# A two-layer graph network on one core: Q and K as three float32r matmuls on split operands, with a new order of events

## What is computed

```python
def euler_step(h, _):
    ax = jnp.einsum('nm,bmd->bnd', adj_mx, h)
    f = alph * 0.5 * (ax - h) + h @ w_eff - h + x0
    return (h + dt * f, None)
...
qkv = h @ W
...
scores = jnp.einsum('bhid,bhjd->bhij', q, k) / np.sqrt(HEAD_DIM) + mask
attn = jax.nn.softmax(scores, axis=-1)
out = jnp.einsum('bhij,bhjd->bhid', attn, v)
...
x = _layernorm(x + _L0_gnn_ref(x, adj, ...), axis=-1)
x = _layernorm(x + _L1_gnn_ref(x, L1_gnn_W, adj), axis=-1)
```

## Time and profile before

| | |
|---|---|
| median of three runs | 652.85 us (652.73 to 653.16) |
| the profiled execution | 653.2 us, its span 651.4 us |
| PE busy | 622.8 us, 96% of the span |
| DVE busy | 520.5 us, 80% |
| ACT busy | 452.5 us, 69% |
| Pool busy | 146.5 us, 22% |
| mean granted TensorE clock | 0.988 of full speed |

### The profile page before, as it was taken

How to read it: one execution, slowest core, us unless ns; L and a number is a source line. 1 busy time by engine, 2 the same in 40 slices (tenths; PEclk the granted TensorE clock), 3 DMA queues, 4 the chain that set the end, 5 groups by cost and what they waited for, 6 DMA issues and landing times.

```text
span 651.4 us, 11315 instructions
## 1 busy us (share of the span) xinstructions
PE 622.8 (96%) x3083; PEld 434.2 (67%) x3083; DVE 520.5 (80%) x1406; ACT 452.5 (69%) x1025; POOL 146.5 (22%) x170
## 2 busy tenths in 40 slices
...
DMA packets 38141, 35.55 MB, mean 55 GB/s; under 512 B 8064, under 2 KB 25312, under 8 KB 38112
## 3 DMA queue, kind: packets, MB, share of 16 engines
...
...
## 4 chain that ended last, share of the span: by engine, by line
PE 87%; DVE 6%; POOL 3%; issue 2%; ACT 1%; DMA 0%; POOLq 0%; SPq 0%; DVEq 0%
PE psL L932 9%; PE psL L933 9%; PE psL L934 9%; PE psE L1032 9%; PE psO L1060 9%; PE psS L946 8%; PE psL L922 5%; PE psL L924 5%; PE psL L923 5%; PE psM L1006 5%; PE psM L1011 2%; PE psL L997 2%; DVE ET L1301 2%; PE psE L848 2%; PE psS L848 2%
## 5 line engine op out<-in xcount | busy, mean ns | idle before, releaser
L1247 DVE CUSTOM_DVE_ANT_0 Sm<-psS,mask 128x512 f32<-128x512 f32 x256 | 172.3, 686 | 30.4 <-PE psS L946 22.6
L737 ACT ACTIVATE Sm<-Sm,negmax 128x512 f32<-128x512 f32 x240 | 171.4, 716 | 24.6 <-DVE negmax L1247 24.1
L1301 DVE TENSOR_TENSOR ET<-psE,maskT 128x512 f32<-128x512 f32 x232 | 154.4, 683 | 13.4 <-PE psE L1032 12.7
L784 ACT ACTIVATE ET<-ET 128x512 f32<-128x512 f32 x240 | 144.2, 620 | 19.3 <-DVE ET L1301 19.1
L946 PE MATMUL psS<-Ks,Qs 96*128 96x512 f32 x256 | 102.4, 432 | 4.6 <-DMA Ks<-kl 2.3
L650 POOL TENSOR_TENSOR rstd<-var,minus_half 128x4 f32<-128x4 f32 x32 | 32.8, 1025 | 307.0 <-DVE var L1230 307.0
L1032 PE MATMUL psE<-Qs,Ks 98*128 98x512 f32 x232 | 94.2, 454 | 2.1 <-DVE ET L1301 0.5
L1032 PEld LDWEIGHTS psE<-Qs,Ks 98*128 98x128 f32 x232 | 42.9, 190 | 33.9 <-issue 13.2
L1060 PE MATMUL psO<-ET,V 128*32 128x512 f32 x512 | 65.4, 608 | 0.0
L946 PEld LDWEIGHTS psS<-Ks,Qs 96*128 96x128 f32 x256 | 48.7, 192 | 20.1 <-issue 6.3
L922 PE MATMUL psL<-z,Rh 128*128 128x512 f32 x144 | 57.6, 400 | 0.0
...
## 6 DMA issues: line engine op xcount, KB each, us to landing
Qs<-qh SPq DMA_DIRECT2D x128, 64.0 KB, 2.0
Ks<-kh SPq DMA_DIRECT2D x128, 64.0 KB, 2.0
...
Qs<-Mh SPq DMA_DIRECT2D x30, 4.0 KB
```

What stands on the lines that cost most here:

```text
L737: nc.scalar.activation(E[:, slot % 2, i, :] if moved(a, h) else row, row, ACT.Exp, scale=-1.0, bias=negmax[:, h * NT + i:h * NT + i + 1], ...
L784: nc.scalar.activation(ET[:, n, i, :], ET[:, n, i, :], ACT.Exp, scale=SCALE).then_inc(st_exp, 1)
L1247: V_.tensor_tensor_reduce(out=Sm[:, i % 2, :], in0=psS[i % 2][:, :], in1=mask[:, i, :], scale=-SCALE, scalar=3e38, op0=ALU.add, op1=ALU.mi ...
L1301: V_.tensor_tensor(ET[:, n, i, :], e_bank(b, n, i)[:, :], maskT[:, i, :], ALU.add).then_inc(t_ev[i % 2], 1)
```

## The change

W's columns for Q and K are split once in the setup into Wh (ACT) and Wl (DVE). The transposed x1 is no longer copied out whole: ACT takes its high part x1Th, DVE its low part x1Tl (a new event XL, which now frees psM for Q), and Q and K are three float32r matmuls each. V still needs the whole x1T: Pool adds it up from the two parts (a new event X1S), and V waits for that. The lists of events are rewritten. Below are the lists of the loop on PE, DVE, Pool and SP, and the code; ACT's list and those for fill and drain are left out.

```diff
...
 PE_EVENTS = [
-    ("TR", 0, 1, 2), ("Z", 1, 0, 0), ("S", 3, 0, 2), ("X1T", 0, 0, 1), ("S", 3, 1, 2), ("TR", 0, 2, 2),
-    ("TR", 0, 3, 2), ("CB", 0, 0, 3), ("Q", 1, 0, 1), ("XT", 0, 0, 0), ("S", 3, 2, 2), ("Z", 2, 0, 0),
-    ("TR", 1, 0, 2), ("K", 2, 0, 1), ("TR", 1, 1, 2), ("TR", 1, 2, 2), ("S", 3, 3, 2), ("C", 2, 0, 0),
-    ("MT", 1, 0, 2), ("TR", 1, 3, 2), ("C", 1, 0, 0), ("S", 0, 0, 1), ("YT", 0, 0, 0), ("S", 0, 1, 1),
-    ("V", 3, 0, 1), ("TR", 2, 0, 2), ("TR", 2, 1, 2), ("S", 0, 2, 1), ("S", 0, 3, 1), ("J", 0, 0, 0),
-    ("TR", 2, 2, 2), ("TR", 2, 3, 2), ("S", 1, 0, 1), ("S", 1, 1, 1), ("TR", 3, 0, 2), ("C", 0, 0, 0),
-    ("S", 1, 2, 1), ("YT", 1, 0, 0), ("S", 1, 3, 1), ("TR", 3, 1, 2), ("TR", 3, 2, 2), ("PV", 0, 0, 2),
-    ("MT", 0, 0, 1), ("TR", 3, 3, 2), ("S", 2, 0, 1), ("S", 2, 1, 1), ("J", 1, 0, 0), ("PV", 1, 0, 2),
-    ("UT", 0, 0, 0), ("S", 2, 2, 1), ("PV", 2, 0, 2), ("PV", 3, 0, 2), ("TR", 0, 0, 1), ("S", 2, 3, 1),
+    ("S", 2, 2, 2), ("TR", 0, 0, 2), ("S", 2, 3, 2), ("Z", 1, 0, 0), ("TR", 0, 1, 2), ("X1T", 0, 0, 1),
+    ("S", 3, 0, 2), ("S", 3, 1, 2), ("TR", 0, 2, 2), ("CB", 0, 0, 3), ("TR", 0, 3, 2), ("XT", 0, 0, 0),
+    ("Q", 1, 0, 1), ("Z", 2, 0, 0), ("TR", 1, 0, 2), ("S", 3, 2, 2), ("K", 2, 0, 1), ("S", 3, 3, 2),
+    ("TR", 1, 1, 2), ("TR", 1, 2, 2), ("C", 2, 0, 0), ("MT", 1, 0, 2), ("C", 1, 0, 0), ("TR", 1, 3, 2),
+    ("S", 0, 0, 1), ("YT", 0, 0, 0), ("S", 0, 1, 1), ("V", 3, 0, 1), ("S", 0, 2, 1), ("TR", 2, 0, 2),
+    ("TR", 2, 1, 2), ("S", 0, 3, 1), ("J", 0, 0, 0), ("TR", 2, 2, 2), ("TR", 2, 3, 2), ("S", 1, 0, 1),
+    ("S", 1, 1, 1), ("TR", 3, 0, 2), ("C", 0, 0, 0), ("S", 1, 2, 1), ("TR", 3, 1, 2), ("S", 1, 3, 1),
+    ("YT", 1, 0, 0), ("TR", 3, 2, 2), ("PV", 0, 0, 2), ("MT", 0, 0, 1), ("TR", 3, 3, 2), ("S", 2, 0, 1),
+    ("S", 2, 1, 1), ("J", 1, 0, 0), ("PV", 1, 0, 2), ("UT", 0, 0, 0), ("PV", 2, 0, 2), ("PV", 3, 0, 2),
 ]
...
 DVE_EVENTS = [
-    ("S", 2, 1, 2), ("LN1A", 0, 0, 1), ("S", 2, 2, 2), ("TR", 0, 0, 2), ("S", 2, 3, 2), ("LN1B", 0, 0, 1),
-    ("TR", 0, 1, 2), ("Z", 1, 0, 0), ("S", 3, 0, 2), ("TR", 0, 2, 2), ("S", 3, 1, 2), ("CB", 0, 0, 3),
-    ("QL", 1, 0, 1), ("S", 3, 2, 2), ("TR", 0, 3, 2), ("XT", 0, 0, 0), ("TR", 1, 0, 2), ("Z", 2, 0, 0),
-    ("KL", 2, 0, 1), ("S", 3, 3, 2), ("TR", 1, 1, 2), ("TR", 1, 2, 2), ("MT", 1, 0, 2), ("LN2A", 0, 0, 3),
-    ("TR", 1, 3, 2), ("S", 0, 0, 1), ("S", 0, 1, 1), ("YT", 0, 0, 0), ("S", 0, 2, 1), ("S", 0, 3, 1),
-    ("TR", 2, 0, 2), ("TR", 2, 1, 2), ("TR", 2, 2, 2), ("S", 1, 0, 1), ("S", 1, 1, 1), ("TR", 2, 3, 2),
-    ("TR", 3, 0, 2), ("S", 1, 2, 1), ("S", 1, 3, 1), ("TR", 3, 1, 2), ("YT", 1, 0, 0), ("MT", 0, 0, 1),
-    ("TR", 3, 2, 2), ("TR", 3, 3, 2), ("S", 2, 0, 1), ("J", 1, 0, 0),
+    ("TR", 0, 0, 2), ("LN1B", 0, 0, 1), ("S", 2, 3, 2), ("TR", 0, 1, 2), ("Z", 1, 0, 0), ("XL", 0, 0, 1),
+    ("TR", 0, 2, 2), ("S", 3, 0, 2), ("TR", 0, 3, 2), ("CB", 0, 0, 3), ("S", 3, 1, 2), ("QL", 1, 0, 1),
+    ("XT", 0, 0, 0), ("TR", 1, 0, 2), ("S", 3, 2, 2), ("KL", 2, 0, 1), ("Z", 2, 0, 0), ("S", 3, 3, 2),
+    ("TR", 1, 1, 2), ("TR", 1, 2, 2), ("MT", 1, 0, 2), ("LN2A", 0, 0, 3), ("TR", 1, 3, 2), ("S", 0, 0, 1),
+    ("S", 0, 1, 1), ("YT", 0, 0, 0), ("S", 0, 2, 1), ("S", 0, 3, 1), ("TR", 2, 0, 2), ("TR", 2, 1, 2),
+    ("TR", 2, 2, 2), ("S", 1, 0, 1), ("TR", 2, 3, 2), ("S", 1, 1, 1), ("TR", 3, 0, 2), ("S", 1, 2, 1),
+    ("S", 1, 3, 1), ("TR", 3, 1, 2), ("YT", 1, 0, 0), ("TR", 3, 2, 2), ("S", 2, 0, 1), ("MT", 0, 0, 1),
+    ("J", 1, 0, 0), ("TR", 3, 3, 2), ("S", 2, 1, 1), ("LN1A", 0, 0, 0), ("S", 2, 2, 1),
 ]
...
 POOL_EVENTS = [
-    ("KEEP", 0, 0, 2), ("LN1A", 0, 0, 1), ("ADD", 0, 0, 3), ("LN2A", 0, 0, 3), ("XS", 0, 0, 0),
+    ("XS", 0, 0, 0), ("LN2A", 0, 0, 3), ("LN1A", 0, 0, 0), ("ADD", 0, 0, 2), ("X1S", 0, 0, 0), ("KEEP", 0, 0, 0),
 ]
...
 SP_EVENTS = [
-    ("STK", 2, 0, 2), ("MT", 0, 0, 2), ("STK", 3, 0, 2), ("XIN", 0, 0, 0), ("OUT", 0, 0, 4), ("STK", 0, 0, 1),
-    ("MT", 1, 0, 2), ("STK", 1, 0, 1),
+    ("STK", 1, 0, 2), ("XIN", 0, 0, 0), ("STK", 2, 0, 2), ("MT", 0, 0, 2), ("STK", 3, 0, 2), ("STK", 0, 0, 1),
+    ("OUT", 0, 0, 4), ("MT", 1, 0, 2),
 ]
...
+        Wh = sb("Wh", [P, 2 * D], F32R)
+        Wl = sb("Wl", [P, 2 * D], F32R)
...
+        x1Th = sb("x1Th", [P, N], F32R)
+        x1Tl = sb("x1Tl", [P, N], F32R)
...
@@ -670,6 +679,11 @@
                             ins = nc.gpsimd.tensor_scalar(y[:, t, :], att[:, t, :], mv[:, 1, t, 0:1],
                                                           rstd[:, 1, t:t + 1], ALU.subtract, ALU.mult)
                         ins.then_inc(y_done, 1)
+                    elif kind == "X1S":
+                        pool.wait_ge(m_ev, MPB * b + 1)
+                        if after_first(b):
+                            pool.wait_ge(m_mm, MPB * b)
+                        nc.gpsimd.tensor_tensor(x1T[:, :], f(x1Th[:, :]), f(x1Tl[:, :]), ALU.add).then_inc(x1t_sum, 1)
                     elif kind == "KEEP":
                         pool.wait_ge(x1_done, b + 1)
                         if not isinstance(b, int) or b > 1:
@@ -723,6 +737,9 @@
                 act.wait_ge(r_ev, q1)
                 nc.scalar.activation(Rh[:, q0:q1, :], Rf[:, q0:q1, 0:D], ACT.Copy).then_inc(rt_hi, 1)
             power_high(2, 2)
+
+            act.wait_ge(in_qkv, 16)
+            nc.scalar.activation(Wh[:, :], W_sb[:, 0:2 * D], ACT.Copy).then_inc(w_hi, 1)
 
             def high(bank_ap, dst):
                 return nc.scalar.activation(dst, bank_ap, ACT.Copy)
@@ -758,7 +775,7 @@
                         nc.scalar.activation(YT[:, :], psL[bank][:, :], ACT.Copy).then_inc(l0_ev[bank], 1)
                     elif kind == "X1T":
                         act.wait_ge(m_mm, MPB * b + 1)
-                        nc.scalar.activation(x1T[:, :], psM[:, :], ACT.Copy).then_inc(m_ev, 1)
+                        high(psM[:, :], x1Th[:, :]).then_inc(x1t_hi, 1)
                     elif kind in ("Q", "K"):
                         act.wait_ge(m_mm, MPB * b + n + 1)
                         if kind == "Q" and after_first(b):
@@ -1003,9 +1020,14 @@
                         last.then_inc(m_mm, 1)
                     elif kind in ("Q", "K"):
                         cols = slice(0, D) if kind == "Q" else slice(D, 2 * D)
-                        mm(psM[:, :], W_sb[:, cols], x1T[:, :], start=True, stop=True).then_inc(m_mm, 1)
+                        if kind == "Q" and isinstance(b, int) and b == 0:
+                            pe.wait_ge(w_lo, 1)
+                        mm(psM[:, :], Wh[:, cols], x1Th[:, :], start=True, stop=False)
+                        mm(psM[:, :], Wl[:, cols], x1Th[:, :], start=False, stop=False)
+                        mm(psM[:, :], Wh[:, cols], x1Tl[:, :], start=False, stop=True).then_inc(m_mm, 1)
                     elif kind == "V":
                         cols = slice(2 * D, 3 * D)
+                        pe.wait_ge(x1t_sum, b + 1)
                         for t in range(NT):
                             nodes = slice(t * P, (t + 1) * P)
                             last = mm(psM[:, nodes], x1T[:, nodes], W_sb[:, cols], start=True, stop=True)
@@ -1209,6 +1231,8 @@
             power_low(2, 2)
             mask_columns(3)
             dve.wait_ge(c_vec, 5 + NT)
+            dve.wait_ge(w_hi, 1)
+            V_.tensor_tensor(Wl[:, :], W_sb[:, 0:2 * D], f(Wh[:, :]), ALU.subtract).then_inc(w_lo, 1)
             V_.memset(y[:, :, :], 0.0).then_inc(y_out, Y_FREE)
             V_.memset(negmax[:, :], 0.0).then_inc(c_ev, C_FREE)
 
@@ -1282,6 +1306,9 @@
                         dve.wait_ge(x1_kept, b)
                         normalise(0, b, lambda t: psM[:, t * P:(t + 1) * P],
                                   lambda t: x1[:, t, :]).then_inc(x1_done, 1)
+                    elif kind == "XL":
+                        dve.wait_ge(x1t_hi, b + 1)
+                        low(psM[:, :], x1Th[:, :], x1Tl[:, :]).then_inc(m_ev, 1)
                     elif kind in ("QL", "KL"):
                         dve.wait_ge(m_hi, (MPB - 2) * b + n)
                         h_, l_ = {"QL": (qh, ql), "KL": (kh, kl)}[kind]
```

22 lines of the change are left out of this document (12 added, 10 removed), and 301 rows, old and new, of tables (ACT_DRAIN, ACT_EVENTS, ACT_FILL, DVE_DRAIN).

## The result

The changed kernel takes 655.29 us (median of 22 executions, 651.82 to 657.58), the kernel before in the same session 653.18 (22 executions, 652.07 to 654.00). The ratio is 1.0025, with a 95% interval of 1.0013 to 1.0037: slower by a quarter of a per cent, where 650.8 us was forecast. The time lies 0.3 us above the range given.

A forecast was written before the change was run, and what follows sets the result against it. PE was taken as the bound, nearly without a stall, with DVE's chain nearly as long. Loop -1.0, fill -0.8, other orders -0.4, loop and drain entries -0.1, drain +0.3: -2.0 us, giving 650.8 us, range 646.5 to 655.0.

The forecast's parts named there:

- Loop: Ten loop batches: DVE's queue eats most of PE's 0.45 us gain, leaving 0.1 a batch; -1.0 us, -2.2 to +1.0.
- the queue from TR(0,1) on: Loop, DVE from TR(0,1) to YT's low part: works without a gap, ends at 21.55 us and sets J's start.
- The kl row of the prediction: Loop, DVE's waits ahead of J: 0.1 us of the vanishing waits left in because kh comes only just in time.
- The rival in which PE alone sets the pace: Loop: DVE stretch too long by 0.3 us or more, period 34.9; -6.5 us, 646.3 us in all, chance 0.15.
- The new waits: Loop: Q for XL (slack 0.1 us), K and C's third part near zero, V for Pool; no cost.
- the third rival: Drain clock: another 5 us at half clock gives 653.3 us, chance 0.10; staying at 2.4 GHz gives 648.3, chance 0.08.
- the second: Loop rival: XL comes on top, no DVE wait goes, J 0.5 us later; +4.1 in all, 656.9 us, chance 0.17.
- Fill: Batch 0: Q starts 0.75 us later, yet J 0.5 earlier and next S group another 0.3; -0.8 us, -1.2 to +0.5.
- Batches 1 to 4: Other written orders: batches 1, 2, 13 and 14 save 0.1 us each as in the loop; -0.4 for all four.
- Drain: Batch 15's chain to S(0,0): XL adds 0.75 us, products take 0.31 out; +0.3 us, with 0 to +0.8.
- The sum: Whole kernel: all terms together -2.0 us on the span of 651.4, 650.8 us against the median of 652.85.

The follow-up runs named there:

- the six shown above: Profiled executions without added fill matmuls whose waits ahead of X1T and Q sum to 2.55 or 2.57 us; four had half clock at 78 to 80 us.
- The added matmuls: Changed kernel plus ten unused float32r matmuls on PE in batch 0, five ahead of X1T and five ahead of Q: 651.59 us, ratio 0.9990.
- the lists alone: Changed kernel's lists with one plain product from x1T each for Q and K, XL and X1S doing nothing: 658.99 us, ratio 1.0099.
- the run with matmuls in the drain alone: Changed kernel plus six unused matmuls ahead of MT(1) of batch 14 and four ahead of S(0,0) of batch 15: 654.68 us, ratio 1.0023.
- the run at full clock up to there: Changed kernel plus ten unused matmuls in batch 0's fill, no half clock ahead of batch 15's S(0,0): 651.59 us, ratio 0.9990.

## Why the prediction was wrong, point by point

**Loop: inside its range, -1.0 forecast for ten batches, -1.6 measured over nine periods.** J was to start 21.35 to 21.7 us after UT, I took 21.5 to 21.6; it starts at 21.39, near the lower end. So a batch gains 0.2 us and not 0.1. Q and K save 0.15 each as worked out, XL costs 0.60, the waits in DVE's stretch went away. That DVE keeps part of PE's gain back was right: 0.45 at kl, 0.21 to 0.26 at J. What I had wrong is the place. It isn't the queue from TR(0,1) on: the run without XL has 0.61 us less in it and the same period. It is K, kh and kl, and then what DVE does behind kl. The kl row of the prediction had it in view ("kh comes only just in time") as a gap of 0.1 and not as the link. The rival in which PE alone sets the pace (34.9 us) is wrong because PE has to wait twice behind kl, at the third part of C and at J.

**The new waits: right, by a hair.** Q's slack was put at 0.1 and is 0.02; the third part of C was due 0.05 us before its input, and it starts 15.39 us after UT, 0.09 late, and loses 0.10 more on its own step. I had PE at J 0.15 to 0.3 us before DVE; these 0.19 us leave 0.02 of it. V waits for nothing. Pool's sum starts 12.47 us after UT and takes 1.29; DVE's rows beside it have their usual 0.68 to 0.69. (Where the prediction speaks there of the third rival, the second is meant.)

**Fill: -0.8 forecast, +1.9 to UT(1). The step that failed.** Q's start was right: 0.75 later forecast, 0.62 measured. But the sum stopped there. It priced XL as a delay, and took for granted that PE goes on at 2.4 GHz behind it. With 2.55 us of waits instead of 1.84, PE came out at 1.2 GHz in the profiled execution, and in four of the six shown above with such waits. I had the clock among the rivals, with 0.18, and looked for it only in the drain, where the kernel before showed it. The added matmuls bring UT(1) back to 102.2 and the ratio from 1.0025 to 0.9990. By the Trainium skill (TensorE: Matmul & The Clock Gate, Part 1) an array that idles is throttled until activity releases it. The windows of the changed kernel agree with it (0.52 behind the waits), and so do those of the run with added matmuls (1.00); two executions with the same waits kept 1.00 without them.

Even at the full clock the 0.8 did not come. UT(1) is then at 102.2, 0.4 behind the kernel before. V behind the second S was to fill a wait and bring J forward by 0.8; the lists alone have UT(1) at 101.8, as before, so that gain did not come at all. XL costs 0.8 us at UT(1) (101.4 without it).

**Batches 1 to 4: -0.2 forecast, +2.1.** I took 0.1 us a batch from the loop without reading these lists. Between UT(1) and UT(4) both kernels have the same matmuls. The kernel before has no wait there that its trace names; the changed one has three, 1.53 us in all: 0.70 for DVE (at 127.28, for ET), 0.19 for a DMA (at 159.26, Ml into Qs) and 0.64 for another (at 193.41, where S waits for kl in Ks). The last comes and goes: the run with matmuls in the drain alone has the same fill, goes without it, and takes 105.8 us instead of 106.5. So 0.7 of the 2.1 us belong to this one execution, and smaller differences between single executions of other runs (106.1 with matmuls in the fill, 105.5 with the old order beside them) can't be told from such scatter. The lists alone take 107.0 there and the old lists with the new products 106.6, the latter with waits of 0.6 to 1.0 us for x1Tl ahead of Q in each of the three batches; without XL the changed lists take 105.1. So XL and the lists both cost here. How the rest is made up stays open.

**Drain: +0.3 forecast, +1.4.** The chain from UT(15) to S(0,0) grew by 0.25 us at the full clock, so the 0.3 was right for it, although the wait for the stacking isn't the 2.3 us I named but 0.88, because MT(1) waits 1.69 ahead of it for att (0.92 and 2.29 in the run at full clock up to there). What failed is the clock again, the mechanism of the third rival: in the profiled execution 3.4 us at half clock lie ahead of S(0,0) and make another 0.65, and 3.4 us more than before in all. The same drain code took 53.7 to 57.0 us as the half clock there varied in amount and place. How many stretches an execution gets there isn't settled by these runs: added matmuls move them and don't remove them for less than they cost.

**The sum.** The forecast was a ratio of 0.9969 (650.8 to 652.85); 1.0025 came, 0.56% or 3.7 us more. As a ratio the upper end of the range was 1.0033, so the size of the miss is one that the range allowed for; the forecast's direction was wrong. Matmuls in the fill take back 0.35% (2.3 us) of it; that they do so through the clock is shown at UT(1) (1.4 us in the profiled execution) and argued for the rest. The remaining 0.21% (1.4 us) lie in the gain of the fill that did not come, in batches 1 to 4 and in the drain, less what the loop gave beyond the forecast. None of the versions that compute the whole output beats the kernel before by more than the measurement tells.
